# Attention layers: the product of probabilities and values moves from the PSUM bank of the queries to the PSUM bank of the keys

## The reference, cut to what matters

```python
h = jnp.maximum(_layernorm(x), 0.0)
x = x + _L0_gnn_ref(h, adj, ...)        # attention: scores + beta*adj, masked where adj <= 0
...                                     # layers 2 and 3, "directed"
h = jnp.maximum(_layernorm(x), 0.0)
x = x + _L3_gnn_ref(h, adj, ...)        # attention: scores*SCALE + adj, rows of zeros dropped, then @ Wo.T + bo

# inside an attention layer, per graph and head
q, k, v = split_heads(h @ Wq + bq), split_heads(h @ Wk + bk), split_heads(h @ Wv + bv)
probs = softmax(q @ k.T * scale + bias)
out = probs @ v
```

## Time and profile before

| | us |
|---|---|
| median of three runs | 2785.4 |
| the profiled execution, span from its first to its last instruction (no other time of it is given) | 2784.9 |
| VectorE busy | 2456.0 (88%) |
| TensorE matmuls busy | 2508.1 (90%) |
| ScalarE busy | 1806.0 (65%) |
| GpSimd busy | 1450.3 (52%) |

### The profile page before, as it was taken

One profiled execution on the slowest core, in us unless ns is written; L12 is line 12 of the kernel. 1 busy time (PEld: TensorE's weight loads), 2 busy tenths in 40 slices (PEclk: granted clock), 3 DMA queues, 4 the chain that ended last, 5 costly groups with the idle time before them and its releaser, 6 DMA issues. The chain is left out here.

```text
span 2784.9 us, 89934 instructions
## 1 busy us (share of the span) xinstructions
PE 2508.1 (90%) x29505; PEld 1866.2 (67%) x29505; DVE 2456.0 (88%) x9771; ACT 1806.0 (65%) x4409; POOL 1450.3 (52%) x2016
## 2 busy tenths in 40 slices
PE   5898898886999998799999999999968998899987
PEld 4888788874666664566666666666557777777776
DVE  6989989886999999688888888888869999999998
ACT  5888888874555554455555555555547777777775
POOL 1223233224777777477777777777633444344433
PEclk9999999998999999799999999999989999999998
DMA  3001011002000000100000000000000000000000
GB/s 104 28 29 30 26 30 30 26 14 88 9 9 9 9 9 6 47 10 9 9 9 10 9 9 9 9 10 9 8 9 25 23 23 26 23 23 23 26 23 23
DMA packets 73989, 60.21 MB, mean 22 GB/s; under 512 B 7888, under 2 KB 73936, under 8 KB 73936
## 3 DMA queue, kind: packets, MB, share of 16 engines
q1 hardware_dynamic: 73936, 59.54, 7.1%
HBM read 46.92 MB, written 12.58 MB: 21 GB/s over the span
## 5 line engine op out<-in xcount | busy, mean ns | idle before, releaser
L149 PE MATMUL bank<-L_w_hi,L_hT_hi 128*128 128x384 f16 x2112 | 691.7, 328 | 0.0
L151 PE MATMUL bank<-L_w_hi,L_hT_lo 128*128 128x384 f16 x2112 | 691.4, 327 | 0.0
L150 PE MATMUL bank<-L_w_lo,L_hT_hi 128*128 128x384 f16 x2112 | 691.4, 327 | 0.0
L550 ACT ACTIVATE raw_weights<-L_minus_scores,L_minus_max 128x128 f32<-128x128 f32 x1536 | 475.7, 389 | 71.2 <-DVE L_minus_max L663 71.2
L149 PE MATMUL bank<-L_hT_hi,L_w_hi 128*128 128x128 f16 x2304 | 418.4, 222 | 1.2 <-issue 0.8
L150 PE MATMUL bank<-L_hT_lo,L_w_hi 128*128 128x128 f16 x2304 | 418.3, 222 | 0.0
L151 PE MATMUL bank<-L_hT_hi,L_w_lo 128*128 128x128 f16 x2304 | 418.1, 222 | 0.0
L663 DVE CUSTOM_DVE_ANT_0 L_minus_scores<-bank,L_minus_score_bias 128x128 f32<-128x128 f32 x1536 | 348.0, 283 | 0.4 <-issue 0.4
L1085 ACT ACTIVATE L_e<-bank,L_nmax 128x128 f32<-128x128 f32 x192 | 70.6, 368 | 365.0 <-DVE L_nmax L1170 365.0
L151 PEld LDWEIGHTS bank<-L_w_hi,L_hT_lo 128*128 128x128 f16 x2112 | 207.4, 98 | 138.2 <-issue 2.5
L150 PEld LDWEIGHTS bank<-L_w_lo,L_hT_hi 128*128 128x128 f16 x2112 | 207.6, 98 | 108.5 <-issue 2.0
(11 more groups left out here) (171 smaller groups left out, 7853.5 us busy)
## 6 DMA issues: line engine op xcount, KB each, us to landing
adj_tile<-in_adj SPq DMA_DIRECT2D x320, 64.0 KB, 1.7
x<-in_x SPq DMA_DIRECT2D x64, 192.0 KB, 2.3
out<-L_result SPq DMA_DIRECT2D x64, 192.0 KB, 1.9
raw_weights<-in_L_gnn_Wq SPq DMA_DIRECT2D x2, 576.0 KB, 4.1
raw_weights<-in_L_gnn_Wk SPq DMA_DIRECT2D x2, 576.0 KB, 5.8
raw_weights<-in_L_gnn_Wv SPq DMA_DIRECT2D x2, 576.0 KB, 5.5
raw_weights<-in_L_gnn_Wl SPq DMA_DIRECT2D x2, 576.0 KB, 4.7
raw_weights<-in_L_gnn_Ws SPq DMA_DIRECT2D x2, 576.0 KB, 4.9
```

What stands on the lines that cost most here:

```text
L149: pe.matmul(out, stat[0], move[0], start=first, stop=False)
L150: pe.matmul(out, stat[0], move[1], start=False, stop=False)
L151: return pe.matmul(out, stat[1], move[0], start=False, stop=last)
L550: last = act.activation(probs[:, n_.slot(k), i, :], scores[:, i, :], ACT.Exp, bias=nmax[:, n_.slot(k), i:i + 1], scale=-1.0)
```

## The change

The product of probabilities and values takes banks[5], the bank of the keys. So the queries of t+1 no longer need `attended(t-2)` and are put right behind the scores, in L3 ahead of `turn_o(t-2)`. The keys of t+1 keep the wait. The product of t-1 now waits for `k_lo(t+1)` where it waited for `q_lo(t+1)`.

```diff
-                pv = banks[4][:, 0:H * (HD + 1)].rearrange("p (h e) -> p h e", h=H)
+                pv = banks[5][:, 0:H * (HD + 1)].rearrange("p (h e) -> p h e", h=H)
...
                             if n_.has(0):
                                 score(n_)
+                            if n_.has(1):
+                                project_turned(n_, 1, 0, q_bank, q_psum)
                             if last_layer and n_.has(-2):
                                 turn_o(n_, -2)
                             if n_.has(1):
                                 wait(pe, attended_ready, n_.done(-2))
-                                project_turned(n_, 1, 0, q_bank, q_psum)
                                 project_turned(n_, 1, 1, k_bank, k_psum)
                             if last_layer and n_.has(-2):
                                 project_out(n_, -2)
...
                                 if n_.has(1):
-                                    wait(pe, q_lo, n_.done(1))
+                                    wait(pe, k_lo, n_.done(1))
                                 wait(pe, attended_ready, n_.done(-2))
                                 attend(n_, -1)
```

## The result

The changed kernel is slower: 2813.86 us (2812.45 to 2815.84, four runs) against 2785.84 us; ratio 1.0103, 95% interval 1.0089 to 1.0118, so + 28.0 us. The forecast was 2805, + 19.6 on its own base, with an own range of 2796 to 2811: the measured time is 2.9 us above that range. The sign, the layer and the stall that makes most of the loss were right. One term of the sum, the low clock, had the wrong sign, and it is most of what is missing. The profiled execution has a span of 2810.8 us, 25.9 above that of before.

The account below looks back on a forecast made before the run. VectorE was taken to pace L3, and a loop through GpSimd and ScalarE to pace L0. L0 cost 0, L3's stall + 21.7 and low clock - 2.0 on 2784.9 gave 2804.6, so 2805 us; own range 2796 to 2811, stated range 2795 to 2814.

Parts of the forecast that it names:

- low clock: L3 steps where TensorE paces: its earlier end gives back nothing to 3.9 us; 2 us taken as gain.
- What bounds each layer: VectorE paces L3, 98% busy; in L0 the loop runs `attended`, GpSimd's sum and norm, ScalarE's `normed`, key split, VectorE.
- rival A: L0: `normed` hangs on TensorE's block, so early queries and keys gain 20.5 us (2784.6) or 54.6 us (2750); 5%.
- L0 at nothing: L0: queries and keys ready about 0.9 us earlier, but ScalarE is in `normed` and nobody takes them; cost 0.
- Exchanged wait and bank at nothing: Both layers: waiting for `k_lo` instead of `q_lo` ahead of `attend(t-1)` costs 0; the banks keep their readers.
- The stall of L3: L3: queries delay `turn_o`, so VectorE waits for `oT_hi` 0.32 or 0.39 us a step, 61 steps, 21.7 us.
- Rival C: L3: queries behind scores wait for more, `turn_o` another 0.2 to 0.3 us late; 36.6 us, 2819; 8%.
- rival B: L3: VectorE's `nonzero_sum` is held less by GpSimd's fold, absorbing the stall; L3 costs nothing, 2783; 7%.
- Sum: Whole kernel: profiled 2784.9 + 21.7 - 2.0 = 2804.6, median 0.5 us above the span, so 2805 us.
- C's own sum: Whole kernel time under the dearer passage in L3: 0.6 us a step, 36.6 us, given as 2819.
- chances of no change: Chance that the whole kernel's measured time shows no change, about 0.2% or 5.6 us: given as 0.08.

Follow-up runs that it names:

- keys-first pair: ScalarE splits keys ahead of `normed` in L0: on the changed kernel with `o_split` behind the eighth head, 2766.33 us; on the kernel before, 2793.94 us.
- kernel with `turn_o` first: Changed kernel with `turn_o` put ahead of the queries again in L3, product still in the keys' bank in both layers: 2782.18 us, ratio 0.9981.
- later split: Changed kernel with VectorE's `o_split` behind the eighth head of the maxima instead of the fourth: 2778.58 us, ratio 0.9961.
- fillers: Extra overwritten matmuls in L3: changed kernel, ahead of `project_v`, four 2806.33 us, two 2805.03 us; kernel before, four ahead of `turn_o`, 2778.17 us.
- four profiles of the old steps: Kernel before; change in L0 alone, 2783.29 us; changed kernel with `turn_o` ahead of queries, 2782.18 us; kernel before with keys ahead of `normed` in L0, 2793.94 us.

## Where the prediction was right, and the term that failed

- **What bounds each layer: right.** VectorE paces L3, the chain `attended`, GpSimd, `normed`, keys paces L0. In both kernels `normed` starts 3.94 us behind `attended` and the split of the keys 4.65 us behind it (medians in L0), although the keys are ready about 0.9 us earlier in the changed one. So rival A, that `normed` hangs on TensorE, is false. The keys-first pair shows ScalarE's place in the chain: only where its order was changed did early keys give much time. That it is GpSimd which releases `normed` is read from the trace; no run tests it.
- **L0 at nothing: nearly.** By the medians 3.7 and 4.8 us were gained in the two timed kernels that have the old order in L3. In the changed kernel's profile the paired steps are 9.07 and 9.16 where 9.10 and 9.16 stood, some 0.9 us over the layer, and the last four take 1.5 us less. The first of these four, 12.09 us before and 10.38 after, has a mean granted clock of 0.87 before and 1.00 after, so a part of that is the clock's. I had looked at the loop and not at the ends. This term went the other way than the miss.
- **Exchanged wait and bank at nothing: right**, by the kernel with `turn_o` first.
- **The stall of L3: right in mechanism and nearly in size.** Rival C, a dearer passage, is false. The passage from scores to queries was put at 0.17 us and is 0.16; queries 1.51, is 1.52; `turn_o` 0.49, is 0.50; the wait of `oT_lo` in the changed kernel ends 0.34 and 0.39 us later, counted from `attended`, where 0.32 and 0.39 were forecast. What the sum lacked is that `oT_lo` itself takes 0.03 us longer: 0.56 us now, 0.52 before. With it 24.1 us were measured for the 21.7 forecast. Why it is longer isn't shown. The wait alone doesn't explain it: with the later split `oT_lo` waits for nothing, follows another instruction, and still takes 0.55 us.
- **Absorbed by GpSimd's hold (rival B): false**, as argued. `nonzero_sum` is 1.02 us long before and 1.03 in the changed kernel (medians in L3), which fits GpSimd having moved with VectorE.
- **Low clock: this term failed.** The forecast was "Bounds: nothing, and 0.97 us in each of some four such steps, 3.9 us; I take 2", as a gain. Measured: a loss of 7.5 us, seven stretches for three, and each dearer, 1.6 us where one cost about 1.2 before. I took the number of stretches as given, and TensorE's earlier end as what VectorE feels in them. But the change moves TensorE's idle time to another place and, through its own stall, makes each step longer with the same work. The fillers show that the stretches hang on that idle time: with it filled they are gone, and 8 us with them. That there are more of them than before (seven, where four profiles of the old steps have 3, 5, 3 and 3) rests on one profile, and why is argued and not shown. They are dearer because the queries, at half speed, now stand ahead of what VectorE waits for: the wait for `oT_hi` is 1.8 to 1.9 us in all seven.
- **Sum**: forecast + 21.7 - 2.0 = + 19.7; by the profiles + 24.1 + 7.5 - 5.05 - 0.6 = + 25.9. So the stall's term was 2.4 us too low and that of the low clock 9.5, and the 5.65 us gained outside took more than half of this back: without that luck the forecast would have been further off. The medians say + 28.0, and two of the four runs had a granted clock of 0.975 and 0.977 against the profiled one's 0.978, and 2815.2 and 2815.8 us. Two small slips of the working change nothing: C's own sum comes to 2820, and the chances of no change add up to 0.09.

## What to carry to other kernels

When a step is moved into an engine's idle time, compare its whole length with that time and not with the idle total: 1.18 us fitted in 1.14 with a slack of 0.11, 1.68 didn't, and all the loss came from the last third. If what is delayed feeds the pacing engine, moving that engine's reader by one place can turn the loss into a gain (1.0103 to 0.9961 here). Work that becomes ready earlier is worth little until its taker's order is changed as well; change both together, and look at the next wait in line.

## What the runs showed of the hardware that I had not expected

- TensorE's granted clock fell to half for some 3.4 us, several times in a layer, although between 2200 and 2700 us it never stood idle for more than 0.94 us at a time in the kernel before and 0.76 in the changed one. Extra matmuls in those gaps took these stretches away and made both kernels faster: 2813.9 to 2805.0 us with two of them a step, and 2786.9 to 2778.2 us for the kernel before with four.
- Matmuls that use 32 rows and then ones that use 128 are 0.16 to 0.17 us apart, where like ones of the same block start 0.056 us apart (the earlier trace rows and the step above).
- The same VectorE instruction, `oT_lo`, lasts 0.52 us directly behind the aggregate of the statistics, 0.56 us behind the same instruction and a wait, and 0.55 us directly behind the read of a maximum, without a wait.
